# Expert operands placed with the stationary blocks 64 bytes behind the moving rows in the first layer and 64 bytes ahead in the second

## What is computed

```python
def reference(x, ...):                        # x: (32, 512, 256) float32
    xn = _layernorm(x)
    return x + attn(xn) + ffn(xn)

# attn: 16 heads of 16; scores = (q k^T) * decay mask (no softmax), out = scores v,
#       projection Wo, then a group norm over each head's (16 x 512) outputs
# ffn (a mixture of 8 experts; every expert chooses its own tokens):
cap = int(2.0 * T / E)                                    # 2 * 512 / 8 = 128
probs = softmax(einsum('BTC,CE->BTE', x, gate_w))
top_p, top_idx = top_k(transpose(probs, (0, 2, 1)), cap)  # 128 tokens for each batch and expert
xin = take_along_axis(x[:, None], top_idx[..., None], 2)
h = gelu(einsum('BElC,ECH->BElH', xin, w1), approximate=False)   # 256 -> 1024
y = einsum('BElH,EHC->BElC', h, w2) * top_p[..., None]           # 1024 -> 256
out = zeros(B, T, C).at[b_idx, top_idx].add(y)
```

## The kernel before, in words

| tensor | role | before, even expert | before, odd expert | after, both |
|---|---|---|---|---|
| w1_hi | stationary, first layer | 0 | 128 | 0 |
| w1_lo | stationary, first layer | 0 | 160 | 0 |
| xs_hi, xs_lo | moving, first layer | 160 | 160 | 64 |
| g_hi, g_lo | stationary, second layer | 160 | 160 | 64 |
| w2_hi | moving, second layer | 128 | 160 | 0 |
| w2_lo | moving, second layer | 128 | 160 and 64 (its two halves) | 0 |
| x_hi, x_lo, a_hi, a_lo (attention) | moving at L1383, x stationary at L1449 | 480 | 480 | 0 |
| w_hi, w_lo, vg_hi (attention) | stationary at L1383, moving at L1449 | 320 | 320 | 0 |

## Time and profile before

### The profile page before, as it was taken

The page is one execution under the profiler, slowest core; times in us unless marked ns, Lnnn a source line. Parts: engine busy times, 40 slices in busy tenths (PEclk is TensorE's granted clock), DMA queues, the critical chain, the costliest instruction groups (busy, mean ns, idle before and its releaser), DMA issues.

```text
span 2338.6 us, 81411 instructions
## 1 busy us (share of the span) xinstructions
PE 2264.5 (97%) x34252; PEld 2095.6 (90%) x34252; DVE 1531.5 (65%) x3103; ACT 1391.5 (59%) x2553; POOL 1283.3 (55%) x2012
## 2 busy tenths in 40 slices
PE   6999999999999988999999999999999999999998
PEld 5777777777777778999999999999999999999998
DVE  3555555656666657996766767667667667676674
ACT  4555565555655546556666656666666666666664
POOL 4444444444544455655566666666566576575453
PEclk9999999999999999999999999999999999999999
DMA  3232222322223312232324324224234233232332
GB/s 120 74 95 85 75 76 83 94 84 76 76 75 94 98 61 71 49 77 50 50 44 89 46 46 91 43 49 86 47 52 82 47 54 80 48 54 43 51 50 33
DMA packets 129368, 157.72 MB, mean 67 GB/s; under 512 B 11008, under 2 KB 118656, under 8 KB 129024
## 3 DMA queue, kind: packets, MB, share of 16 engines
q0 software_dynamic: 49152, 67.14, 17.8%
q1 hardware_dynamic: 79872, 85.54, 11.6%
HBM read 85.53 MB, written 67.11 MB: 65 GB/s over the span
## 4 chain that ended last, share of the span: by engine, by line
PE 55%; DVE 0%; POOL 0%; issue 0%; ACT 0%; DVEq 0%
PE attn L1779 28%; PE scores L1698 18%; PE front L1698 7%; PE front L1688 2%; POOL out L798 0%; DVE rows L211 0%; DVE topi L207 0%; DVE top L202 0%; DVE hidden L1263 0%; DVE xs_lo L1233 0%; ACT res L949 0%; DVE rows L223 0%; PE scores L233 0%; PE scores L232 0%; DVE rows L225 0%
## 5 line engine op out<-in xcount | busy, mean ns | idle before, releaser
L1779 PE MATMUL attn<-w_hi,g_hi 128*128 128x256 f32 x2048 | 581.5, 284 | 2.5 <-DVE g_lo L1274 2.4
L1779 PE MATMUL attn<-w_lo,g_hi 128*128 128x256 f32 x2048 | 578.3, 282 | 0.0
L1779 PE MATMUL attn<-w_hi,g_lo 128*128 128x256 f32 x2048 | 578.1, 282 | 0.0
L987 ACT ACTIVATE hidden<-hidden 128x512 f32<-128x512 f32 x384 | 235.4, 629 | 263.9 <-DVE hidden L1263 263.9
L1779 PEld LDWEIGHTS attn<-w_hi,g_hi 128*128 128x128 f32 x2048 | 388.6, 190 | 3.0 <-DVE g_lo L1274 2.7
L1779 PEld LDWEIGHTS attn<-w_hi,g_lo 128*128 128x128 f32 x2048 | 388.3, 190 | 0.0
L1779 PEld LDWEIGHTS attn<-w_lo,g_hi 128*128 128x128 f32 x2048 | 388.0, 189 | 0.0
L1698 PE MATMUL scores<-xs_hi,w_hi 128*128 128x256 f32 x1280 | 362.0, 283 | 8.4 <-DVE xs_lo L1233 6.3
L1698 PE MATMUL scores<-xs_lo,w_hi 128*128 128x256 f32 x1280 | 362.8, 283 | 0.0
L1263 DVE TENSOR_TENSOR hidden<-front,hidden 128x512 f32<-128x512 f32 x256 | 176.3, 689 | 284.0 <-PE front L1698 270.7
L1698 PE MATMUL scores<-xs_hi,w_lo 128*128 128x256 f32 x1280 | 361.0, 282 | 0.0
(11 more groups left out here) (182 smaller groups left out, 5154.4 us busy)
## 6 DMA issues: line engine op xcount, KB each, us to landing
x<-in_x SPq DMA_DIRECT2D x32, 512.0 KB, 5.3
w_stage<-in_w SPq DMA_DIRECT2D x16, 1024.0 KB, 6.4
xn_rows<-xn SPq DMA_DIRECT2D x32, 512.0 KB, 3.2
res<-in_x SPq DMA_DIRECT2D x32, 512.0 KB, 3.8
out<-res SPq DMA_DIRECT2D x32, 512.0 KB, 3.4
xg<-xn_rows,step_idx POOLq DMA_INDIRECT x256
out<-y,scatter_idx POOLq DMA_INDIRECT x128, 3.9
out<-res,scatter_idx POOLq DMA_INDIRECT x128, 3.9
```

The lines of the kernel that those rows point to most:

```text
L987: act.activation(own(q, p), src, ACT.Gelu).then_inc(g_ready, 1)
L1779: last = pe.matmul(yb[k % 2][:, 0:D], g_[:, m, cols], w, start=start and m == first and i == 0, stop=end, skip_group_check=True)
```

## The change

It touches only where tensors lie. The expert operands get bases for which the stationary block lies 64 bytes behind the moving rows, modulo 512, in the first layer, and 64 bytes ahead in the second, for even and odd experts alike (the table above). To make room, the small tensors of layer norm and group norm and the two index tensors are allocated first, and the large buffers of the attention part get fixed offsets too, nearly all on whole KB. The instructions, their order, their shapes, the DMAs and the waits are the same.

```diff
+        gst_w = sb("gate_stage", [P, DH, E])
+        st = sb("ln_stats", [P, TT, 6])
...
+        idx = sb("step_idx", [P, GRP], U32)
+        sidx = sb("scatter_idx", [P, GRP], U32)
         route = Routing(ctx, nc, cst)
...
-        w_hi = [None if i == 2 else sb(f"w_hi{i}", [P, DH, D], F32R) for i in range(4)]
-        w_lo = [sb(f"w_lo{i}", [P, DH, D], F32R) for i in range(4)]
...
-        x_hi = sb("x_hi", [P, DH, S], F32R)
-        x_lo = sb("x_lo", [P, DH, S], F32R)
...
+        KB = 1024
+        w_hi = [None if i == 2 else at(f"w_hi{i}", [P, DH, D], F32R, o * KB)
+                for i, o in enumerate((54, 56, None, 58))]
+        w_lo = [at(f"w_lo{i}", [P, DH, D], F32R, (60 + 2 * i) * KB) for i in range(4)]
+        vg_hi = at("vg_hi", [P, DH, VG], F32R, 80 * KB)
...
+        x_hi = at("x_hi", [P, DH, S], F32R, 143 * KB)
+        x_lo = at("x_lo", [P, DH, S], F32R, 147 * KB)
...
+        a_hi = at("a_hi", [P, DH, S], F32R, 171 * KB)
+        a_lo = at("a_lo", [P, DH, S], F32R, 175 * KB)
...
-        LATE = 186880
-        w1h = [at("w1_hi0", [P, 7, QF], F32R, LATE), at("w1_hi1", [P, 7, QF], F32R, 56448)]
-        w1l = [at("w1_lo0", [P, 7, QF], F32R, LATE + K1), at("w1_lo1", [P, 7, QF], F32R, 167584)]
-        s2 = at("w2_stage", [P, FT, D], F32, LATE + 2 * K1)
-        w2h = [at("w2_hi0", [P, FT, D], F32R, 78976), at("w2_hi1", [P, FT, D], F32R, 106144)]
+        G_AT = 87 * KB + 64
+        X_AT = 143 * KB + 64
+        w1h = [at("w1_hi0", [P, 7, QF], F32R, 183 * KB + 512), at("w1_hi1", [P, 7, QF], F32R, 57 * KB)]
+        w1l = [at("w1_lo0", [P, 7, QF], F32R, 197 * KB + 512), at("w1_lo1", [P, 7, QF], F32R, 169 * KB + 512)]
+        s2 = at("w2_stage", [P, FT, D], F32, 211 * KB + 512)
+        w2h = [at("w2_hi0", [P, FT, D], F32R, 79 * KB), at("w2_hi1", [P, FT, D], F32R, 157 * KB + 512)]
         w2l = [[at(f"w2_lo{i}{j}", [P, FT // 2, D], F32R, o) for j, o in enumerate(os)]
-               for i, os in enumerate(((70784, 74880), (181920, LATE + 2 * K1 + K2 + 1088)))]
+               for i, os in enumerate(((71 * KB, 75 * KB), (165 * KB + 512, 219 * KB + 512)))]
...
-        xs_hi = at("xs_hi", [P, 7, HALF], F32R, 87712)
-        xs_lo = at("xs_lo", [P, 7, HALF], F32R, 87712 + KX)
...
-        g_hi = at("g_hi", [P, FT, SL], F32R, 134816)
-        g_lo = at("g_lo", [P, FT, SL], F32R, 151200)
+        g_hi = at("g_hi", [P, FT, SL], F32R, G_AT)
+        g_lo = at("g_lo", [P, FT, SL], F32R, G_AT + FT * SL * 4)
...
+        xs_hi = at("xs_hi", [P, 7, HALF], F32R, X_AT)
+        xs_lo = at("xs_lo", [P, 7, HALF], F32R, X_AT + 7 * HALF * 4)
```

More of the change, by code:

```diff
@@ L254, in layer @@
         vec = sb("vec", [P, V_N])
+        gst_w = sb("gate_stage", [P, DH, E])
+        st = sb("ln_stats", [P, TT, 6])
+        mv = sb("ln_mv", [P, TT, 2])
+        ln_ve, ln_r, ln_y, ln_a, ln_m = (sb(f"ln_{n}", [P, TT]) for n in ("ve", "r", "y", "a", "m"))
+        ost = sb("o_stats", [P, DH, 6])
+        gm = sb("g_moments", [P, DH, 2])
+        gs = sb("g_means", [P, DH, 2])
+        gn_ve, gn_r, gn_y, gn_a, gn_m, gn_s, gn_b = (sb(f"gn_{n}", [P, DH])
+                                                     for n in ("ve", "r", "y", "a", "m", "s", "b"))
+        idx = sb("step_idx", [P, GRP], U32)
+        sidx = sb("scatter_idx", [P, GRP], U32)
         route = Routing(ctx, nc, cst)
@@ L261, in layer @@
         wst = s1[:, 0:4, :].rearrange("p a (b n) -> p (a b) n", n=D).rearrange("p (i h) n -> p i h n", h=DH)
-        gst_w = sb("gate_stage", [P, DH, E])
-        bv = sb("bv_rows", [P, D])
-        w_hi = [None if i == 2 else sb(f"w_hi{i}", [P, DH, D], F32R) for i in range(4)]
-        w_lo = [sb(f"w_lo{i}", [P, DH, D], F32R) for i in range(4)]
[L267 to L270, removed]
@@ L271, in layer @@
-        st = sb("ln_stats", [P, TT, 6])
-        mv = sb("ln_mv", [P, TT, 2])
-        ln_ve, ln_r, ln_y, ln_a, ln_m = (sb(f"ln_{n}", [P, TT]) for n in ("ve", "r", "y", "a", "m"))
-        x_hi = sb("x_hi", [P, DH, S], F32R)
-        x_lo = sb("x_lo", [P, DH, S], F32R)
[L276 to L289, removed]
@@ L290, in layer @@
-        gn_ve, gn_r, gn_y, gn_a, gn_m, gn_s, gn_b = (sb(f"gn_{n}", [P, DH])
-                                                     for n in ("ve", "r", "y", "a", "m", "s", "b"))
+        KB = 1024
+        bv = at("bv_rows", [P, D], F32, 53 * KB)
+        w_hi = [None if i == 2 else at(f"w_hi{i}", [P, DH, D], F32R, o * KB)
+                for i, o in enumerate((54, 56, None, 58))]
+        w_lo = [at(f"w_lo{i}", [P, DH, D], F32R, (60 + 2 * i) * KB) for i in range(4)]
+        xb = [at(f"x{i}", [P, TT, D], F32, (68 + 4 * i) * KB) for i in range(2)]
@@ new lines, in layer @@
+        xn = at("xn", [P, TT, D], F32, 76 * KB)
+        vg_hi = at("vg_hi", [P, DH, VG], F32R, 80 * KB)
+        vraw = at("v_unbiased", [P, TT, VG], F32, 80 * KB + DH * VG * 4)
+        tm = [at(f"state{i}", [P, NSUB - 1, DH, 2 * HD], F32, 90 * KB - (2 - i) * (NSUB - 1) * DH * 2 * HD * 4)
+              for i in range(2)]
+        kn = at("k_natural", [P, TT, D], F32, 90 * KB)
+        k32 = [at(f"k{i}", [P, DH, S], F32, o * KB) for i, o in enumerate((127, 94))]
+        qd = [at(f"q_decayed{i}", [P, DH, S], F32, o * KB) for i, o in enumerate((131, 98))]
@@ new lines, in layer @@
+        qm = [at(f"q_parity{i}", [P, DH, 2, S], F32, o * KB) for i, o in enumerate((135, 102))]
+        vm = [at(f"v_parity{i}", [P, TT, VW], F32, 110 * KB + i * TT * VW * 4) for i in range(2)]
+        x_hi = at("x_hi", [P, DH, S], F32R, 143 * KB)
+        x_lo = at("x_lo", [P, DH, S], F32R, 147 * KB)
+        q32 = at("q32", [P, DH, S], F32, 151 * KB)
+        s_sb = [at(f"s_sb{i}", [P, PAIRS, 512], F32, (155 + 8 * i) * KB) for i in range(2)]
+        a_hi = at("a_hi", [P, DH, S], F32R, 171 * KB)
@@ L293, in layer @@
+        a_lo = at("a_lo", [P, DH, S], F32R, 175 * KB)
+        o32 = at("o32", [P, DH, S], F32, 179 * KB)
         tb = ctx.enter_context(nc.psum_tensor("front", [P, DH, 512], F32))
@@ L382, in layer @@
         HALF = SL // 2
-        K1 = 7 * QF * 4
-        K2 = FT * D * 4
-        KX = 7 * HALF * 4
-        LATE = 186880
-        w1h = [at("w1_hi0", [P, 7, QF], F32R, LATE), at("w1_hi1", [P, 7, QF], F32R, 56448)]
-        w1l = [at("w1_lo0", [P, 7, QF], F32R, LATE + K1), at("w1_lo1", [P, 7, QF], F32R, 167584)]
-        s2 = at("w2_stage", [P, FT, D], F32, LATE + 2 * K1)
-        w2h = [at("w2_hi0", [P, FT, D], F32R, 78976), at("w2_hi1", [P, FT, D], F32R, 106144)]
-        w2l = [[at(f"w2_lo{i}{j}", [P, FT // 2, D], F32R, o) for j, o in enumerate(os)]
-               for i, os in enumerate(((70784, 74880), (181920, LATE + 2 * K1 + K2 + 1088)))]
@@ L393, in layer @@
-        xg = [at(f"xg{k}", [P, D], F32, 53248 + 1024 * k if k < 3 else LATE + 2 * K1 + K2) for k in range(GRP)]
-        idx = at("step_idx", [P, GRP], U32, LATE + 2 * K1 + K2 + 1024)
-        sidx = at("scatter_idx", [P, GRP], U32, LATE + 2 * K1 + K2 + 1056)
-        xs_hi = at("xs_hi", [P, 7, HALF], F32R, 87712)
-        xs_lo = at("xs_lo", [P, 7, HALF], F32R, 87712 + KX)
-        xsum = at("x_sums", [P, 4, HALF], F32, 87712 + 2 * KX)
-        hid = {q: at(f"hidden{q}", [P, 2, 2, HALF], F32, o)
-               for q, o in (("22", 114336), ("21", 118432), ("11", 122528), ("12", 130720))}
@@ L401, in layer @@
-        y = [at("y", [P, GRP, D], F32, 126624), res]
-        g_hi = at("g_hi", [P, FT, SL], F32R, 134816)
-        g_lo = at("g_lo", [P, FT, SL], F32R, 151200)
+        G_AT = 87 * KB + 64
[3 more added lines that the diff above has]
+        s2 = at("w2_stage", [P, FT, D], F32, 211 * KB + 512)
@@ new lines, in layer @@
+        w2h = [at("w2_hi0", [P, FT, D], F32R, 79 * KB), at("w2_hi1", [P, FT, D], F32R, 157 * KB + 512)]
+        w2l = [[at(f"w2_lo{i}{j}", [P, FT // 2, D], F32R, o) for j, o in enumerate(os)]
+               for i, os in enumerate(((71 * KB, 75 * KB), (165 * KB + 512, 219 * KB + 512)))]
+        xg = [at(f"xg{k}", [P, D], F32, (53 + k) * KB) for k in range(GRP)]
+        g_hi = at("g_hi", [P, FT, SL], F32R, G_AT)
+        g_lo = at("g_lo", [P, FT, SL], F32R, G_AT + FT * SL * 4)
+        hid = {q: at(f"hidden{q}", [P, 2, 2, HALF], F32, G_AT + o * KB)
+               for q, o in (("22", 32), ("21", 36), ("11", 44), ("12", 48))}
@@ L405, in layer @@
+        y = [at("y", [P, GRP, D], F32, G_AT + 40 * KB), res]
+        xsum = at("x_sums", [P, 4, HALF], F32, G_AT + 52 * KB)
+        xs_hi = at("xs_hi", [P, 7, HALF], F32R, X_AT)
+        xs_lo = at("xs_lo", [P, 7, HALF], F32R, X_AT + 7 * HALF * 4)
         xb_ = {p: sbk[:, i, :] for i, p in enumerate("AB")}
```

## The result

The changed kernel takes 2310.83 us in the median (2309.13 to 2315.53), the kernel before 2346.76 us beside it: a ratio of 0.985, 95% interval 0.983 to 0.987, or 36 us less. The profiled executions took 2309.13 and 2340.57 us, 31.4 us apart; the rest lies in the runs around them: the profile of before was 6 to 7 us under its median, that of after 1.7.

A forecast was written before the change was run, and what follows sets the result against it. TensorE was taken as the bound, by matmul count times pitch. From 2347.25 us, -7.6 (even steps), -11.9 (odd), -1.4 (first eight), +0.9 (seams) and +3.3 (attention) sum to -16.7, giving 2331 us; range 2298 to 2363.

The forecast's parts named there:

- The variable: Expert matmuls: pitch depends on the loaded block's distance from the streaming row, modulo 512 bytes; 0 costs 1.7 ns over 32.
- The value for distance 64: Late expert steps, 170 pairs each: pitch 116.6 ns, extrapolated from distances 0 and 32; gains 7.6 us (even) and 11.9 us (odd).
- The seams: Between the expert layers, nine pairs a step fall on distance 0: 0.9 us lost.
- The first eight steps: First eight expert steps: VectorE taken as the fuller engine, so half of 8 x 0.35 counted, 1.4 us gained.
- The attention part: Attention matmuls move from distance 160 to 0: 1920 pairs at +1.7 ns, 3.3 us lost.
- A: Both expert layers: distance counts only modulo 64 bytes, so 64 is as bad as 0; +18.0 us, 2365 us; chance 0.25.
- B: Expert steps: nothing but distance 0 is special; even steps stay, odd fall to 22.15 us; 2347 us; chance 0.22.
- C: Expert steps: at 64 bytes the reads stop meeting, pitch about 114 ns, step about 21.4 us; 2304 us; chance 0.15.
- Even and odd experts now alike: Chain of the changed kernel: even and odd expert steps should have the same length, 21.9 us.
- 2.68 us for 23 pairs: Timeline of the second expert layer: 23 pairs should take 2.68 us.
- Ten 512-column pairs: Attention part: ten such pairs should take 2.33 to 2.36 us; less would mean its term is wrong in sign.
- step 4: Attention part: x_hi, a_hi and all w and vg buffers go from distance 160 to 0; 3.3 us lost.

The follow-up runs named there:

- d0: Changed kernel with xs and g on whole KB (x = 0, x being their bytes past a whole KB): distance 0 in both layers; 2353.91 us, 1.0037 of before.
- all32_d64: Changed kernel with every expert operand moved 32 bytes on, distances kept at 64; 2315.75 us, step 21.713 us.
- allbehind: Changed kernel re-based so the loaded block lies 64 bytes behind the streaming rows everywhere, in both layers and at all seams; 2327.51 us, 0.994 of before.
- allahead: Changed kernel re-based so the loaded block lies 64 bytes ahead of the streaming rows everywhere, in both layers and at all seams; 2329.21 us, 0.994 of before.
- seam64: Changed kernel with w2 and g moved 64 bytes on, modulo 256: distance 64 at the layer seams too, instead of 0; 2293.48 us, 0.980 of before.
- seam192: Changed kernel with second-layer weights and g moved: still 64 inside both layers, but 192 (64 to the other side modulo 256) at the seams; 2301.12 us.
- x = 96: Changed kernel with xs and g 96 bytes past a whole KB instead of 64; 2338.55 us, step 22.340 us.
- x = 224: Changed kernel with xs and g 224 bytes past a whole KB instead of 64; 2327.53 us, mean step 22.091 us.
- att160: Changed kernel with the attention part's streamed tiles 160 bytes further on, back at distance 160, experts still at 64; 2306.71 us, 0.986 of before.
- x = 256: Changed kernel with xs and g 256 bytes past a whole KB instead of 64; 2347.71 us, step 22.460 us.
- x = 192: Changed kernel with xs and g 192 bytes past a whole KB instead of 64; 2314.84 us, step 21.818 us.
- 448: Changed kernel with xs and g 448 bytes past a whole KB instead of 64, exchanging the two layers' signs; 2318.33 us, step 21.818 us.

## Why the prediction was wrong in size

The direction and the place were right: faster, in the steady expert steps, by the pitch alone, with no wait in the place of another. 2331 us was forecast, 2310.8 came, inside the range; -16.7 us was forecast and -36 came. Of the 19 us between them the pairs and seams of the late steps hold 8.4 (forecast -19.5 + 0.9, measured -27.0), the first eight steps 3.1, the attention part 2.6, the end 0.6, and the runs around the two profiled ones 4.5. Step by step:

**The variable.** Distance, and not the alignment or the new neighbours: right, by d0 and all32_d64. Modulo 512: 256 is enough.

**The value for distance 64 is the step that failed, and it failed twice over.** I drew a line through 0 and 32 and took 116.6 ns for all 170 pairs. There is no such pitch. Distance 64 with nothing switching gives 117.8 (allbehind, allahead), so the term was too large: a step of 22.080 instead of 22.218 is 7.6 us over 55 steps, where 28 x 0.27 + 28 x 0.425 = 19.5 was counted. On top of that comes a short rhythm of 113.3 ns which no row of before showed over a run of pairs, and which some seams turn on: 22.080 - 21.727 = 0.353 us a step, 19.4 us. Together 27.0.

**The seams.** Counted as nine pairs on a bad distance, 0.9 us lost. They are where those 19.4 us come from: the sign was wrong, because I priced a seam as a pair and not by what it does to the pairs behind it. That the seams pay is shown by seam64, seam192, allbehind and the changed kernel, which all have 64 inside the layers and 21.52, 21.70, 22.08 and 21.73 us.

**The first eight steps.** Counted by half, -1.4 us, measured -4.5. The reason for the half was a misreading: the earlier trace rows have VectorE busy for 164.0 us and TensorE for 172.9, so VectorE was not the fuller one (and the row runs from 860 to 1052, where the eight steps run from 870.9 to 1073.7). Eight times the whole 0.49 us of a step would be 3.9, but that the pitch gave the 4.5 isn't shown: over the traces of all kernels this stretch takes 196.1 us (x = 96, step 22.340) to 206.2 (x = 224, step 22.091), and at distance 0, where a late step is longer than any of before (22.460 us), it takes 201.4, less than the 202.8 of before. Among its waits, the 2.4 us wait for g_lo is gone, the one for xs_lo is 6.8 instead of 6.3.

**The attention part.** Counted +3.3, with +1.7 ns for distance 0. The sign of the pitch was wrong: 512-column pairs got faster, 2.26 us for ten, and L1383 as a whole fell from 291.7 to 286.3 us, counted from each matmul's start to the next one's (by the same count L1563 rose from 33.6 to 38.9, with more idle time ahead of it). Yet the experts began 0.7 us later. The changed kernel was 6.1 us ahead at its last round of attention (826.7 against 832.8 us), but att160, with the slower pitch of 234.2 ns, was too (826.6), so that isn't the pitch's doing. The last round and what follows it, up to the experts, took 44.9 us instead of 38.1. The two rows, before and after:

```profile
832.80:870.90 38.10, 32.49 (x882) 26.14 (x879) 22.84 (x61) 16.28 (x30) 16.80 (x32) 0.96 0.28 86
```

```profile
826.70:871.60 44.90, 33.64 (x882) 27.03 (x879) 26.96 (x61) 16.55 (x30) 16.76 (x32) 0.89 0.24 73
```

The same 882 matmuls, TensorE idle 11 us instead of 6, and a granted clock of 0.89 instead of 0.96: from 855.7 to 865.5 us it was at the lower level, 1.2 GHz, through a wait of 5.0 us for `state`. The 18 kernels with this attention part start their experts anywhere between 861.9 us (x = 224) and 877.0 (x = 0), and the last round takes 40.5 to 41.4 us in eleven of them and 44.9 to 45.6 in seven; x = 0 has 45.3 where x = 256, with the same step, has 41.1. So I don't put the whole 6.8 us down to the change; the 2.4 by which even the shortest is over the 38.1 of before, known from one trace, stay open.

**The rivals.** A (64 as bad as 0): refuted by d0, 22.460 against 21.727; its 22.46 us a step is what distance 0 gives, to the last digit. B (only 0 is special): closest for one distance of 64 everywhere, 22.080 against its 22.15, and what allbehind would have looked like; not for this kernel. C (the reads stop meeting, 114 ns): half right, and nearer in the kernel's time than my forecast, though not in the step (21.73 us; C 21.4, mine 21.9). Half of the pairs run at 113.3: 96 and 84 of 180, in turn, by the chain. I had set C low because the single pitches of 0.11 us in the earlier trace rows stood beside 0.13.

**The signs named in advance.** Even and odd experts now alike: yes, but steps differ in turn by 0.035 us, by the rhythm they begin in. 2.68 us for 23 pairs: neither, 24 take 2.73 or 2.83, which is 2.6 or 2.7 for 23. Ten 512-column pairs in 2.26 us: the sign of step 4 was wrong, as the text said it would mean. No late wait of TensorE: right.

**The two rules.** The Trainium skill, "SBUF — State Buffer", "Who interferes with whom", has independent ports and a TensorE that never waits. This case disagrees: d0 and the changed kernel differ in nothing but the place of operands, by 0.73 us in each step (22.460 and 21.727). At which part of the path the two reads get in each other's way no run shows. The gap rule of "TensorE: Matmul & The Clock Gate", "Back-to-back issue gap", 109.2 ns for 256 columns, is given there for a matmul by itself, and for pairs with a weight load the same section says that both set the spacing. It isn't reached here: the short rhythm is 113.3, in every kernel where it occurs.

**Open.** Why two rhythms exist at 64 bytes, why a seam from behind to ahead turns one into the other, and what the transposes leave behind (each becomes the other in the changed kernel, short becomes long in seam64, long becomes short in seam192, short stays short in all32_d64, each at every step). If the 54 long pairs of seam64 ran short, its step would be 54 x 4.5 ns = 0.24 us shorter, 21.28 us.

## What to carry to other kernels

Where TensorE is full and nothing waits, the place of the operands is still a lever: compare the address of the block that is loaded with that of the row that streams, modulo 256 bytes, and for pairs of 256 columns keep away from 0 and from 96 behind (here 120.0 and 119.9 against 117.8 ns a pair at 64). Then read the chain of waits piece by piece, since a mean pitch can hide two rhythms, and try the seams between products as well as their inside: here they were worth 0.56 us of a step of 22.08 (allbehind against seam64), more than going from 0 to 64 everywhere, 0.38 (22.460 to 22.080). Don't interpolate between two measured distances; one run with a base moved tells more.

## What the runs showed of the hardware

- The distance counts modulo 256 bytes: x = 0 and 256 give the same step, 22.460 us, and x = 192 and 448 too, 21.818.
- A run of pairs of 256 columns with a 128-column load has at distance 64 two stable rhythms, 113.3 and 117.8 ns. Within a layer a run of pairs, up to 42 long, doesn't change it once its first few pairs are past, and it is carried across some seams. Other distances inside the layers (0, 32, 96, 128) showed 116.6 to 120.1 ns in the runs of twelve and more, and never the short one.
- At distance 0 the weight loads of the expert steps are longer, 192 to 193 ns in the mean instead of 188 to 189 in the changed kernel (groups of instructions of d0, weight loads):

```profile
L1779 PEld LDWEIGHTS attn<-w_lo,g_hi 128*128 128x128 f32 x2048 | 392.7, 192 | 0.0
L1698 PEld LDWEIGHTS scores<-xs_lo,w_hi 128*128 128x128 f32 x1280 | 247.3, 193 | 0.0
```

- With 512 columns distance 0 is better than 160, 228.5 ns in the mean against 234.1 at 160: the rule of the 256-column pairs doesn't carry over to another shape.
